# Six state-space layers rewritten around the scan: four products of a unit on VectorE, four on GpSimd

## The reference, cut to what matters

```
xz = rmsnorm(x) @ in_w ;  u, z = split(xz)
uc = silu(conv4(u) + cb)
x_dbl = uc @ xp_w ;  dt_r, B, C = split(x_dbl)     # 16, 16, 16
dt = softplus(dt_r @ dt_w + dt_b) ;  A = -exp(A_log)
h_t = exp(dt_t * A) * h_(t-1) + (dt_t * u_t) * B_t  # 16 states
y_t = sum over states of h_t * C_t
x = x + ((y + uc * D) * silu(z)) @ out_w
```

## Time and profile before

| what | value |
|---|---|
| runs: median (lowest to highest) | 408.72 us (407.43 to 410.31), 3 runs |
| the profiled execution: span | 409.9 us |
| mean granted clock of TensorE | 0.926 of full speed |
| first and last `dbu` product of VectorE (L1121), units 0 and 11 | 157.5 and 363.3 us |

### The profile page before, as it was taken

One profiled execution on the slowest core, in us unless ns is written; L12 is line 12 of the kernel. 1 busy time (PEld: TensorE's weight loads), 2 busy tenths in 40 slices (PEclk: granted clock), 3 DMA queues, 4 the chain that ended last, 5 costly groups with the idle time before them and its releaser, 6 DMA issues.

```text
span 409.9 us, 5884 instructions
## 1 busy us (share of the span) xinstructions
PE 340.5 (83%) x1818; PEld 235.1 (57%) x1818; DVE 314.7 (77%) x538; ACT 249.1 (61%) x681; POOL 210.6 (51%) x235
## 2 busy tenths in 40 slices
PE   5868998999899986888887979888888879768674
PEld 3356765565584654566664757566566647557442
DVE  2674678898653618779999799979988999998653
ACT  2012378888727455948778586948676786862170
POOL 1985000000000028788889698868977797882000
PEclk9985999999979997899999899899989999987868
DMA  7900000000002105142450515161342326050000
GB/s 238 403 7 1 2 1 2 0 2 2 0 2 64 40 4 206 44 165 75 173 178 31 208 43 205 29 220 62 144 162 86 123 86 210 3 203 0 2 0 13
DMA packets 11345, 35.24 MB, mean 86 GB/s; under 512 B 2368, under 2 KB 2992, under 8 KB 11192
## 3 DMA queue, kind: packets, MB, share of 16 engines
q1 hardware_dynamic: 11032, 34.61, 23.9%
q10 hardware_dynamic: 288, 0.33, 0.3%
HBM read 34.54 MB, written 0.39 MB: 85 GB/s over the span
## 4 chain that ended last, share of the span: by engine, by line
PE 53%; DVE 24%; ACT 12%; issue 5%; DMA 3%; POOL 2%; DVEq 0%; SPq 0%; POOLq 0%; ACTq 0%
PE PS L664 15%; DVE big L1133 7%; ACT PS L1405 4%; PE PS L511 4%; PE PS L643 3%; DVE big L1121 3%; DVE big L1140 3%; PE PS L475 2%; ACT sg L1368 2%; PE PS L289 2%; PE PS L295 2%; PE PS L627 2%; PE PS L405 2%; PE PS L575 2%; PE PS L485 2%
## 5 line engine op out<-in xcount | busy, mean ns | idle before, releaser
L1133 DVE TENSOR_TENSOR_SCAN big<-PS,big 128x1024 f32<-128x1024 f32 x48 | 109.3, 2284 | 3.0 <-ACT PS L1405 2.7
L664 PE MATMUL PS<-big,cst 128*128 128x256 f32 x384 | 96.0, 407 | 0.0
L1405 ACT ACTIVATE PS<-dt,amat 128x255 f32<-128x255 f32 x192 | 80.1, 466 | 25.4 <-DVE dt L1105 21.5
L1611 POOL TENSOR_TENSOR big<-dtu,big 128x1024 f32<-128x1024 f32 x36 | 84.2, 2356 | 7.2 <-DVE dtu L1108 6.6
L664 PEld LDWEIGHTS PS<-big,cst 128*128 128x128 f32 x384 | 76.8, 205 | 14.9 <-issue 3.7
L1644 POOL TENSOR_SCALAR lnv<-mv 128x4 f32<-128x4 f32 x1 | 0.4, 418 | 93.9 <-DVE mv L770 93.9
L1140 DVE TENSOR_TENSOR big<-big,PS 128x1024 f32<-128x1024 f32 x36 | 43.8, 1216 | 0.9
L1239 ACT ACTIVATE big<-PS 128x512 f32<-128x512 f32 (+1 forms) x43 | 24.8, 584 | 22.3 <-PE PS L511 7.3
L643 PE MATMUL PS<-stack,pick_b 96*128 96x256 bf16 x144 | 23.9, 292 | 17.0 <-DVE big L1140 9.2
L1286 ACT ACTIVATE big<-PS,big 128x256 f32<-128x256 f32 x64 | 29.8, 475 | 1.5 <-DVE big L902 1.5
L1619 POOL TENSOR_TENSOR big<-big 128x1024 f32<-128x1024 f32 x12 | 28.3, 2358 | 1.1 <-DVE big L1133 1.1
(11 more groups left out here) (309 smaller groups left out, 624.6 us busy)
## 6 DMA issues: line engine op xcount, KB each, us to landing
big<-spill SPq DMA_DIRECT2D x48, 512.0 KB, 5.6
wmt<-in_wm SPq DMA_DIRECT2D x6, 418.0 KB, 3.2
w3t<-in_w SPq DMA_DIRECT2D x1, 1588.0 KB, 13.5
big<-routed SPq DMA_DIRECT2D x8, 128.0 KB, 3.0
w2t<-in_w SPq DMA_DIRECT2D x1, 896.0 KB, 10.1
cst<-in_const SPq DMA_DIRECT2D x1, 848.0 KB, 8.0
w5t<-in_w SPq DMA_DIRECT2D x1, 812.0 KB, 15.0
w1t<-in_w SPq DMA_DIRECT2D x1, 385.0 KB, 8.4
```

The lines of the kernel that those rows point to most:

```text
L664: last = pe.matmul(yps, ident, hc[:, g, s], start=False, stop=(g == NSG - 1 and s == SG - 1))
L1133: v.tensor_tensor_scan(flat(hst[g][:]), flat(da[g % 2]), flat(dbu[:, g]), 0.0, ALU.mult, ALU.add).then_inc(sem("m_h"), 1)
L1405: one = act.activation(da[g % 2][:, n, 1:N], dt[b][:, 1:N], ACT.Exp, scale=amat[k][:, col:col + 1])
L1611: pool.tensor_tensor(dbu[:, g], dtu[b][:].unsqueeze(1).to_broadcast([P, SG, N]), bsp[b][:, SG * (g - 1):SG * g], ALU.mult).then_inc(sem("m ...
```

## The change

The mixer is rewritten; the network before and after it stays, but for setup work. In words, with the core of the diff behind it:

- Products: VectorE now makes dbu of groups 0 and 1 and hc of groups 2 and 3 (the last in two halves); GpSimd makes dbu of groups 2 and 3 and hc of groups 0 and 1. Each had four large products per unit before and has four now.
- Spreading: `replicate` makes a set with 32-bit operands straight from xds. Each of its four matmuls uses 32 rows, alternately partitions 0 to 31 and 32 to 63, into banks 4 and 5. There are still four sets per unit. The three-part split, `stack` and `pick_b` go.
- dt comes from uc by one product matrix (x_proj times dt_proj, made once), without the way over xds. Biases enter as an extra bfloat16 matmul of 96 rows at the start of an accumulation. sigmoid's halving is folded into uc (tanh + 1), and factors of 0.5 into weights and copies.
- softplus: six ScalarE operations and three VectorE ones in SBUF, none on GpSimd.
- The residual sum is made by TensorE in `out_proj` (identity times Y, in front of the two projection matmuls); ScalarE takes squares and the scaled copy from PSUM and copies Y back (`keep_residual`). The scaling by the rate goes from GpSimd to ScalarE (`prep_hs`).
- The transposed input takes 64 rows twice (a transposition and a matmul by the identity into the upper half, shifted by one column), and one ScalarE copy instead of two.
- `keep_awake(3)` of each unit goes. All 12 units are written out; the hardware loops go.
- Weights of all six layers are loaded at the start, in pieces, and kept in SBUF; setup is made once: six transpositions and six small matmuls on TensorE with three copies on ScalarE around L351 and L372, and splitting of the biases, conv weights, rates and D on GpSimd after L1537. The two `spare(7, 2)` at L351 and L372 go.

```diff
--- before.py
+++ after.py
+            def prep_transpose(u):
+                b = u % 2
                 pe.wait_ge(sem("m_hs"), u + 1)
+                pe.matmul(PS[64:128, 7, 0:1], zero_t[:], ident[:, 0:1], start=True, stop=True)
                 for a in range(HALF):
...
+                    pe.transpose(PS[0:64, 7, a * P:(a + 1) * P], hs2[b][:, a, 0:D], ident)
+                    last = pe.matmul(PS[64:128, 7, 1 + a * P:1 + (a + 1) * P], hs2[b][:, a, 0:D], ident, start=True, stop=True)
                 last.then_inc(sem("m_tr"), 1)
...
+            def prep_in(u):
+                i, b = divmod(u, 2)
+                pe.wait_ge(sem("m_ht"), u + 1)
+                pe.matmul(ups, bias[:, i, :, 0], ones[:], start=True, stop=False)
+                pe.matmul(ups, wcv[:, i, 0], ht[b][:, 3:3 + N], start=False, stop=False)
+                pe.matmul(ups, wcv[:, i, 1], ht[b][:, 1:1 + N], start=False, stop=True).then_inc(sem("m_in"), 1)
+                pe.matmul(zps, inz[:, i], ht[b][0:64, 3:3 + N], start=True, stop=True).then_inc(sem("m_in"), 1)
+            def prep_x(u):
+                i, b = divmod(u, 2)
                 pe.wait_ge(sem("m_uc"), u + 1)
...
+                pe.matmul(dtp, bias[:, i, :, 1], ones[:], start=True, stop=False)
+                pe.matmul(dtp, wdt[:, i], uc[b], start=False, stop=True)
+                pe.matmul(xd, wxd[:, i], uc[b], start=True, stop=True).then_inc(sem("m_xd"), 1)
+            def replicate(u, first):
+                b = u % 2
+                for s in range(2):
+                    for c in range(2):
+                        r = slice(32 * c, 32 * c + 32)
+                        col = first + 2 * c + s
+                        last = pe.matmul(PS[:, 4 + c, s * N:(s + 1) * N], pick[r, col:col + 1].to_broadcast([32, P]),
+                                         xds[b][r], start=True, stop=True)
+                last.then_inc(sem("m_BC"), 1)
+            def spread_first(u):
                 pe.wait_ge(sem("m_xds"), u + 1)
...
+                pe.wait_ge(sem("m_hc3"), 2 * u)
+                replicate(u, 0)
+            def spread_second(u):
+                pe.wait_ge(sem("m_dbu"), 2 * u + 1)
+                replicate(u, SG)
+            def spread_third(u):
+                pe.wait_ge(sem("m_dbu"), 2 * u + 2)
+                replicate(u, DS + 2 * SG)
+            def spread_last(u):
+                pe.wait_ge(sem("m_hc2"), u + 1)
+                replicate(u, DS + 3 * SG)
...
+            def sum_last(u):
+                for h in range(2):
+                    pe.wait_ge(sem("m_hc3"), 2 * u + h + 1)
+                    for s in range(2 * h, 2 * h + 2):
+                        last = pe.matmul(yps, ident, hc[:, NSG - 1, s], start=False, stop=(s == SG - 1))
+                last.then_inc(sem("m_y"), 1)
...
+            def out_proj(u):
+                i, b = divmod(u, 2)
+                if u + 1 < UNITS:
+                    pe.wait_ge(sem("m_dt"), u + 2)
+                if u >= 2:
+                    pe.wait_ge(sem("m_ycp"), u - 1)
+                pe.matmul(hidp, ident, Y[:, :, b], start=True, stop=False)
                 pe.wait_ge(sem("m_gate"), u + 1)
                 for a in range(HALF):
...
+                    last = pe.matmul(hidp[:, a], yg[b][:, a * P:(a + 1) * P], wout[:, i], start=False, stop=(a == HALF - 1))
                 last.then_inc(sem("m_hid"), 1)
...
-                    keep_awake(3)
...
+            keep_awake(7, 6)
+            prep_transpose(0)
+            keep_awake(1)
+            pe.wait_ge(sem("m_weights"), 5)
+            prep_in(0)
+            keep_awake(3)
+            prep_x(0)
             keep_awake(7)
...
+            for u in range(UNITS):
+                more = u + 1 < UNITS
+                if u:
+                    sum_last(u - 1)
+                spread_first(u)
+                if u:
+                    out_proj(u - 1)
+                spread_second(u)
+                if more:
+                    prep_transpose(u + 1)
+                    prep_in(u + 1)
+                spread_third(u)
+                if more:
+                    prep_x(u + 1)
+                sum_skip(u, u + 1 if more else None)
+                sum_y(u, 0)
+                spread_last(u)
+                sum_y(u, 1)
+                sum_y(u, 2)
+            sum_last(UNITS - 1)
+            out_proj(UNITS - 1)
...
+            def prep_uc(u):
+                v.wait_ge(sem("m_tu"), u + 1)
+                v.scalar_tensor_tensor(uc[u % 2], tu[u % 2], 1.0, ups, ALU.add, ALU.mult).then_inc(sem("m_uc"), 1)
+            def prep_dt(u):
+                b = u % 2
+                v.wait_ge(sem("m_sp"), 6 * u + 4)
+                v.scalar_tensor_tensor(sp_a, sp_3, LOG_D2, sp_u, ALU.add, ALU.mult).then_inc(sem("m_poly"), 1)
+                v.wait_ge(sem("m_sp"), 6 * u + 6)
+                v.wait_ge(sem("m_poly"), 2 * u + 1)
+                v.scalar_tensor_tensor(sp_v, sp_2, LOG_SCALE * LOG_D, sp_a, ALU.add, ALU.mult).then_inc(sem("m_poly"), 1)
+                v.wait_ge(sem("m_poly"), 2 * u + 2)
+                v.scalar_tensor_tensor(dt[b], dtp, 0.0, sp_v, ALU.max, ALU.add).then_inc(sem("m_dt"), 1)
+                v.wait_ge(sem("m_dt"), u + 1)
+                v.wait_ge(sem("m_uc"), u + 1)
+                v.scalar_tensor_tensor(dtu[b], dt[b], 0.5, uc[b], ALU.mult, ALU.mult).then_inc(sem("m_dtu"), 1)
...
+            def drive(u, g):
+                v.wait_ge(sem("m_BC"), 4 * u + g + 1)
+                if g == 0:
+                    v.wait_ge(sem("m_dtu"), u + 1)
+                v.tensor_tensor(dbu[:, g], dtu[u % 2].unsqueeze(1).to_broadcast([P, SG, N]), BCv, ALU.mult)\
+                    .then_inc(sem("m_dbu"), 1)
...
+            def weigh_third(u):
+                v.wait_ge(sem("m_h"), u * NSG + 3)
+                v.wait_ge(sem("m_BC"), 4 * u + 3)
+                v.tensor_tensor(hc[:, 2], hst[:, 2], BCv, ALU.mult).then_inc(sem("m_hc2"), 1)
+            def weigh_last(u):
+                g = NSG - 1
+                v.wait_ge(sem("m_h"), u * NSG + g + 1)
+                v.wait_ge(sem("m_BC"), 4 * u + 4)
+                for h in range(2):
+                    s = slice(2 * h, 2 * h + 2)
+                    v.tensor_tensor(hc[:, g, s], hst[:, g, s], BCv[:, s], ALU.mult).then_inc(sem("m_hc3"), 1)
+            prep_uc(0)
+            for u in range(UNITS):
+                prep_dt(u)
+                if u:
+                    gate(u - 1)
+                drive(u, 0)
+                scan(u, 0)
+                drive(u, 1)
+                scan(u, 1)
+                if u + 1 < UNITS:
+                    prep_uc(u + 1)
+                scan(u, 2)
+                weigh_third(u)
+                scan(u, 3)
+                weigh_last(u)
...
+            def prep_hs(u):
+                b = u % 2
+                act.wait_ge(sem("m_rms"), u)
+                for a in range(HALF):
+                    last = act.activation(hs2[b][:, a, 0:D], hidp[:, a] if u >= 2 else Y[:, a, b], ACT.Copy,
+                                          scale=rms[b][:, a:a + 1])
+                last.then_inc(sem("m_hs"), 1)
...
+            def prep_softplus(u):
+                act.activation(sp_a, dtp, ACT.Abs).then_inc(sem("m_sp"), 1)
+                act.wait_ge(sem("m_sp"), 6 * u + 1)
+                act.activation(sp_u, sp_a, ACT.Exp, scale=-1.0).then_inc(sem("m_sp"), 1)
+                act.activation(sp_v, sp_a, ACT.Tanh, scale=0.5, bias=turn_t).then_inc(sem("m_sp"), 1)
+                act.wait_ge(sem("m_sp"), 6 * u + 3)
+                act.activation(sp_3, sp_u, ACT.Square, bias=a2_t).then_inc(sem("m_sp"), 1)
+                act.activation(sp_1, sp_v, ACT.Square, bias=a_t).then_inc(sem("m_sp"), 1)
+                act.wait_ge(sem("m_sp"), 6 * u + 5)
+                act.activation(sp_2, sp_1, ACT.Square, scale=LOG_ROOT, bias=b_t).then_inc(sem("m_sp"), 1)
...
+            every = range(SG)
+            for u in range(UNITS):
+                more = u + 1 < UNITS
+                decay(u, 0, every)
+                if u:
+                    act.wait_ge(sem("m_hid"), u)
                 else:
...
+                    act.wait_ge(sem("ln_norm"), 7)
+                if more:
+                    prep_norm(u + 1)
+                if u:
+                    keep_residual(u - 1)
+                decay(u, 1, every[0:2])
+                if more:
+                    prep_hs(u + 1)
+                decay(u, 1, every[2:4])
+                if more:
+                    prep_ht(u + 1)
+                decay(u, 2, every[0:3])
+                if more:
+                    prep_tu(u + 1)
+                decay(u, 2, every[3:4])
+                if more:
+                    prep_zs(u + 1)
+                decay(u, 3, every)
+                if more:
+                    prep_xd(u + 1)
+                    prep_softplus(u + 1)
+                    prep_z(u + 1)
...
+            def weigh(u, g):
+                pool.wait_ge(sem(f"ld_C{u % 2}{g}"), 16 * (u // 2 + 1))
```

(15 more changed lines are left out.)

596 lines of the change are left out of this document (197 added, 399 removed).

## The result

The changed kernel takes 481.6 us (median of 4 runs, 480.8 to 482.8) against 408.7 for the kernel before on the same chip: a ratio of 1.181, 95% interval 1.173 to 1.189. Ratios are formed from the runs in the faster of the two states that an execution can take, so they can differ a little from the quotient of the medians. The forecast was 414.0, between 401 and 422. The side was right, the size was not: +73 us in place of +5.4.

What follows compares the result with a forecast made beforehand. No engine was always busy; VectorE and TensorE end the unit. Units +4.7, entry -2.6, last unit's tail +1.5, behind the gate +0.4, setup +1.4 make +5.4 us on the profiled 409.9; on the 408.72 median, 414.0, range 401 to 422.

Steps and rivals of the forecast that it cites:

- The clock: TensorE early in each unit: granted clock falls to 0.50 in nine units of ten for some 3.4 us, costing 0.85 mean.
- Unit 0: First mixer unit: squares behind the first exponentials and GpSimd's first product after 0 make uc later, so 20.0 us.
- A unit at full clock: One mixer unit, first product to next, without a clock fall: grows from 17.8 to 18.3 us.
- The road I put second: Path within a unit from uc through x_dbl, dt, skip and group 0 sums to the tail: 18.0 us, against 18.3.
- The set: Four 32-bit matmuls of 32 rows on TensorE: 1.06 us start to start, 1.17 until the result can be read.
- sets that don't overlap: Rival: a set's matmuls don't pair, a set takes 1.73 us, units 20.0, +16, 425 us in all; chance 0.09.
- The rival in which the clock stays up: TensorE stays at 1.00 through a unit's first 5 us: units 18.3, together 202.3, total 405 or 401; chance 0.29.
- GpSimd's first product late: Rival: B's broadcast comes late, so power and uc do too, some 1.3 us 12 times: +15, 424 us; chance 0.07.
- Setup: Work ahead of the scaled input: fillers go, small matmuls come, VectorE slows beside GpSimd; +1.4 us, between 0 and 3.
- Entry: Scaled input to first product: new chain takes 10.45 us in place of 13.06, so -2.6 us.
- the end: Last unit and the rest: longer tail +1.5 us, identity matmul and ScalarE copy behind the gate +0.4; +1.9 together.

## Why the prediction was wrong

- **The step that failed** is in "The clock": a fall "for some 3.4 us as in the earlier trace rows", costing 0.85 a unit that it meets. That it falls at the start, in nearly every unit, came true, in eleven of eleven, though the start was fuller than I put it (3.36 us busy of 4.98 in place of 2.0 of 3.8). Its length didn't: 10.24 us in eight units, 13.65 in two, 17.07 in unit 0. Of 10.24 us at half speed, 5.1 are lost, and as TensorE is the bound and without a gap there, all of it shows: (266.3 - 27.1) / 10 = 23.9 a unit against 18.97 with the clock held. I took the length of a low stretch from a kernel with fillers and 96-row sets, and carried it over to one with neither; without the fillers that kernel's own low stretches are 6.8 to 10.2. What keeps the clock low for 10 us in which TensorE hardly pauses, no run shows beyond that. The range took the error over, as no rival let the stretch last. The price was low too: in the kernel before a fall of 3.4 us makes a unit 1.8 longer.
- **Unit 0** was forecast at 20.0 and measured 27.1, by the same step.
- **A unit at full clock**, forecast 18.3, is 18.97 (with fillers that fit their gaps). The road I put second ("uc at 7.5, then x_dbl and dt 1.0, skip 0.4, sums of group 0 1.7, and the same tail, gives 18.0") binds: these take 1.2, 0.54 and 1.8, and TensorE reaches them at 7.8. The last set starts 11.35 into the unit, 0.6 behind the third product with C.
- **The set** of four, 1.06 from start to start, came out as in the earlier trace rows: 280.07 to 281.13, where the sums follow. That rival, sets that don't overlap, is out.
- **The rival in which the clock stays up** didn't come by itself. Three fillers made its condition true, and with unit 0 mended eleven units took 208.7 us, or 204.5 without the skip term on TensorE, where it had 202.3.
- **GpSimd's first product late** didn't come: it starts at 260.76, 3.2 us ahead of VectorE's first product; uc's wait of 0.58 is for the tanh behind input matmuls at half clock.
- **Setup**, +1.4, was +8.5. I had the contention and priced it at 0.2 an operation, from an operation of 256 columns beside GpSimd instructions of 0.95 us. Here GpSimd's instructions last 3 us, and an operation is held until such a one ends. I also let the work fall into the attentions; it began at 35 us, on the path. Put off, it gave back 4.2 us at the attention's start; given to VectorE, 4.8 at the scaled input. The other 3.7 of the 8.5 are open. TensorE's clock was low at the setup for 17.07 us, against 13.65 before; no run tells whether that is the rest.
- **Entry**, -2.6, was -1.3, and **the end**, +1.9, was +2.2. The second is partly luck: the same end was 2.9 shorter in the run with the setup work on VectorE, where one low stretch fewer met it.

## What to carry to other kernels

A low stretch of TensorE's clock has no fixed length or price (3.4 to 17 us here, for 1.8 to 5 us a unit and more in unit 0), so it can't be carried over from a kernel whose fillers or wide matmuls the change takes out. Where a sparse stretch of TensorE repeats, one 128-row filler in each gap is worth a try: here it fitted the gaps and gained more than any edit of the real work. One-time work on GpSimd with long instructions is to be kept from beside VectorE's work in SBUF; here it was best on VectorE itself, in its waits.

## What was not expected of the hardware

- Matmuls of the same length and order, over gaps of 0.5 to 0.7 us, held TensorE's clock with 128 rows (a fall in one of eleven units), partly with 64 (four), and not with 32 (eleven).
- TensorE stayed at 0.50 for 10.24 us while it was busy for 10.21 of them.
- GpSimd instructions of 1.5 to 3.4 us held VectorE operations with a single tensor input in SBUF as well: 4.75 us for two that took 0.62, and 3.20 for one of 0.42 with two inputs; those that read PSUM kept their time (0.66 and 0.28).
